# Adding at the destination: one of three folds in a feature-crossing kernel becomes a DMA

## What is computed

```python
x0 = xk = e                                   # (1024, 39, 16)
for W in (f0, f1, f2):                        # (39*39, 128), (128*39, 128), (128*39, 128)
    z = einsum('bfd,bgd->bfgd', x0, xk).reshape(b, f * g, d)
    xk = einsum('bpd,pm->bmd', z, W)          # (1024, 128, 16)
    outs.append(xk)
z = sum(concatenate(outs, axis=1), axis=-1)   # (1024, 384)
h = concatenate([z, dense_ctx], axis=1)       # (1024, 400)
h = maximum(h @ W_top1 + b_top1, 0); h = maximum(h @ W_top2 + b_top2, 0)
y = h @ W_top3
```

## Time and profile before

| | |
|---|---|
| median of 3 runs | 1478.6 us (1476.04 to 1482.9) |
| span of the profiled execution | 1472.1 us (its own time beyond the span is not given) |
| busy: VectorE, ScalarE, GpSimd | 1171.3, 954.1, 1150.0 us |
| chain that ended last, by engine | PE 44%, issue 16%, DVE 15%, POOL 14%, DMA 5% |
| mean granted TensorE clock | 0.966 of full speed (2.4 GHz) |

### The profile page before, as it was taken

One profiled execution on the slowest core, in us unless ns is written; L12 is line 12 of the kernel. 1 busy time (PEld: TensorE's weight loads), 2 busy tenths in 40 slices (PEclk: granted clock), 3 DMA queues, 4 the chain that ended last, 5 costly groups with the idle time before them and its releaser, 6 DMA issues.

```text
span 1472.1 us, 25210 instructions
## 1 busy us (share of the span) xinstructions
PE 1312.5 (89%) x5987; PEld 1044.1 (71%) x5987; DVE 1171.3 (80%) x3210; ACT 954.1 (65%) x3077; POOL 1150.0 (78%) x834
## 2 busy tenths in 40 slices
PE   0259998998989998999989999899989999899998
PEld 0127776786767876788777877688767887788777
DVE  2028998967988698978988699887988789896993
ACT  1117786756766586766867577666867578675783
POOL 7655889977889788978899788997899787674772
PEclk9959999999999999999999999999999999999999
DMA  8132213402233023232133222330233320330200
GB/s 213 19 59 56 48 22 74 79 8 51 51 69 61 3 51 64 59 57 48 19 66 65 37 51 57 64 60 3 52 61 60 57 51 19 74 76 5 49 1 1
DMA packets 62703, 74.33 MB, mean 50 GB/s; under 512 B 25835, under 2 KB 32988, under 8 KB 62538
## 3 DMA queue, kind: packets, MB, share of 16 engines
q1 hardware_dynamic: 52554, 69.88, 22.9%
q0 software_dynamic: 9984, 2.58, 2.0%
HBM read 59.74 MB, written 4.96 MB: 44 GB/s over the span
## 4 chain that ended last, share of the span: by engine, by line
PE 44%; issue 16%; DVE 15%; POOL 14%; DMA 5%; ACT 4%; SPq 1%; another core or an unknown queue 1%; DVEq 1%; ACTq 0%; POOLq 0%
PE pieces L699 10%; PE pieces L701 9%; PE pieces L700 9%; DVE parts L540 9%; POOL emb L311 4%; POOL parts L320 4%; DMA partners<-x_wide 4%; PE xbank L719 3%; ACT parts L406 3%; PE gbank L710 3%; POOL parts L322 2%; DVE pairs L550 2%; PE cur_bank L681 2%; DVE pairs_lo L566 2%; PE cur_bank L682 2%
## 5 line engine op out<-in xcount | busy, mean ns | idle before, releaser
L406 ACT ACTIVATE parts<-pieces,x_cols 128x128 f32<-128x128 f32 x2560 | 721.0, 377 | 193.2 <-PE pieces L701 167.7
L540 DVE SCALAR_TENSOR_TENSOR parts<-pieces,x_cols,parts 128x128 f32<-128x128 f32 x2432 | 679.0, 340 | 141.4 <-PE pieces L701 106.3
L699 PE MATMUL pieces<-w_hi,cur_hi 128*128 128x512 f32 (+1 forms) x1280 | 550.2, 430 | 64.8 <-DVE parts L540 53.1
L701 PE MATMUL pieces<-w_hi,cur_lo 128*128 128x512 f32 (+1 forms) x1280 | 500.5, 391 | 0.0
L700 PE MATMUL pieces<-w_lo,cur_hi 128*128 128x512 f32 (+1 forms) x1280 | 499.7, 390 | 0.0
L320 POOL TENSOR_TENSOR parts<-parts 128x1024 f32<-128x1024 f32 x127 | 325.0, 2559 | 129.8 <-DVE parts L540 127.8
L311 POOL DMA_INDIRECT emb<-in_tbl,next_ids x312 | 325.5, 1043 | 92.4 <-issue 79.8
L699 PEld LDWEIGHTS pieces<-w_hi,cur_hi 128*128 128x128 f32 x1280 | 244.9, 191 | 133.9 <-DVE parts L540 69.3
L420 ACT ACTIVATE pairs_hi<-pairs 117x512 fp32r<-117x512 f32 (+1 forms) x224 | 142.0, 634 | 231.7 <-DVE pairs L550 194.7
L701 PEld LDWEIGHTS pieces<-w_hi,cur_lo 128*128 128x128 f32 x1280 | 243.5, 190 | 50.6
L700 PEld LDWEIGHTS pieces<-w_lo,cur_hi 128*128 128x128 f32 x1280 | 245.2, 192 | 47.1 <-issue 0.4
(11 more groups left out here) (67 smaller groups left out, 712.3 us busy)
## 6 DMA issues: line engine op xcount, KB each, us to landing
partners<-x_wide SPq DMA_DIRECT2D x62, 546.0 KB
partners<-x_wide SPq DMA_DIRECT2D x31, 468.0 KB
x_cols<-emb_rows SPq DMA_DIRECT2D x128, 59.0 KB
emb<-in_tbl,next_ids POOLq DMA_INDIRECT x312
x_wide<-x_rep SPq DMA_DIRECT2D x31, 156.0 KB
wt<-in_wt SPq DMA_DIRECT2D x1, 768.0 KB
wt<-in_wt SPq DMA_DIRECT2D x1, 512.0 KB
partners<-in_w SPq DMA_DIRECT2D x1, 351.0 KB
```

Source lines behind the costliest of these rows:

```text
L406: last = nc.scalar.activation(parts[n % 2][:, 4 * i + r, :], src[:, r * H:(r + 1) * H], ACT.Copy, scale=x_cols[n // 4][:, n % 4, f:f + 1])
L540: nc.vector.scalar_tensor_tensor(acc, src[:, r * H:(r + 1) * H], x_cols[n // 4][:, n % 4, f:f + 1], acc, ALU.mult, ALU.add).then_inc(acc_d ...
L699: nc.tensor.matmul(dst[:, 0:width], hi[:, cols], w1_hi[:, ws], start=True, stop=False)
L701: nc.tensor.matmul(dst[:, 0:width], lo[:, cols], w1_hi[:, ws], start=False, stop=True).then_inc(l2d_ready if q in D_PIECES else l2a_ready, 1)
```

## The change

The addition of 8 onto 8 leaves GpSimd's compute list. In its place GpSimd issues a DMA with an addition at the destination, from `parts[8:16]` to `parts[0:8]`: 128 rows of 4096 bytes. An addition of one number in a scratch buffer stands between the wait for the parts and the issue. The list of a block is now: wait for the parts, issue the fold, gathers, `make_x_diag`, wait for the fold's landing, the two other additions, once a quad the move. `tree_done` counts two additions a block. The last block keeps its addition on VectorE, with a semaphore of its own.

```diff
-TREE = 3
+TREE = 2
...
+        scratch = sb("scratch", [P, 2])
...
-            def add_parts(u, n):
-
-                g, v, out4 = u * BLOCKS + n, parts[n % 2], tails[n % 2]
+            def fold_parts(u, n):
+
+                g, v = u * BLOCKS + n, parts[n % 2]
                 pool.wait_ge(prod_done, (g + 1) * len(A_PIECES))
                 pool.wait_ge(acc_done, (g + 1) * D_OPS)
-                pool.tensor_tensor(v[:, 0:8], v[:, 0:8], v[:, 8:16], ALU.add).then_inc(tree_done, 1)
-                pool.wait_ge(tree_done, g * TREE + 1)
+                pool.tensor_tensor(scratch[:, 0:1], scratch[:, 0:1], scratch[:, 1:2], ALU.add)
+                pool.dma_start(v[:, 0:8], v[:, 8:16], accum_op=ALU.add).then_inc(parts_folded, 16)
+
+            def add_parts(u, n):
+
+                g, v, out4 = u * BLOCKS + n, parts[n % 2], tails[n % 2]
+                pool.wait_ge(parts_folded, (g + 1) * 16)
                 pool.tensor_tensor(v[:, 0:4], v[:, 0:4], v[:, 4:8], ALU.add).then_inc(tree_done, 1)
                 wait(pool, cur2_ready, g - 1)
-                pool.wait_ge(tree_done, g * TREE + 2)
+                pool.wait_ge(tree_done, g * TREE + 1)
                 pool.tensor_tensor(out4[:], v[:, 0:4], v[:, 16:20], ALU.add).then_inc(tree_done, 1)
...
+            pool.memset(scratch[:], 0.0)
...
+                    fold_parts(u, n)
                     for f in shares:
                         gather(u + 1, f)
+                    make_x_diag(u, n)
                     add_parts(u, n)
                     if k == 0 and not last:
                         pool.wait_ge(gathered, (u + 1) * F * 16)
                         pool.wait_ge(rows_copied, u + 1)
                         move_ids(u + 1)
-                    make_x_diag(u, n)
...
             for n in range(BLOCKS - EARLY, BLOCKS - 1):
+                fold_parts(QUADS - 1, n)
+                make_x_diag(QUADS - 1, n)
                 add_parts(QUADS - 1, n)
-                make_x_diag(QUADS - 1, n)
...
-                nc.vector.tensor_tensor(v[:, 0:8], v[:, 0:8], v[:, 8:16], ALU.add).then_inc(tree_done, 1)
-                dve.wait_ge(tree_done, g * TREE + 1)
+                nc.vector.tensor_tensor(v[:, 0:8], v[:, 0:8], v[:, 8:16], ALU.add).then_inc(last_folded, 1)
+                dve.wait_ge(last_folded, 1)
```

More of the change, by code:

```diff
@@ L192, in cin_kernel @@
         prod_done = sem("prod_done")
+        parts_folded = sem("parts_folded")
+        last_folded = sem("last_folded")
         tree_done = sem("tree_done")
@@ L313, in gather @@
                     bass.IndirectOffsetOnAxis(ap=next_ids[:, f:f + 1], axis=0)).then_inc(gathered, 16)
+            def fold_parts(u, n):
+                g, v = u * BLOCKS + n, parts[n % 2]
+                pool.wait_ge(prod_done, (g + 1) * len(A_PIECES))
+                pool.wait_ge(acc_done, (g + 1) * D_OPS)
+                pool.tensor_tensor(scratch[:, 0:1], scratch[:, 0:1], scratch[:, 1:2], ALU.add)
+                pool.dma_start(v[:, 0:8], v[:, 8:16], accum_op=ALU.add).then_inc(parts_folded, 16)
             def add_parts(u, n):
                 g, v, out4 = u * BLOCKS + n, parts[n % 2], tails[n % 2]
-                pool.wait_ge(prod_done, (g + 1) * len(A_PIECES))
-                pool.wait_ge(acc_done, (g + 1) * D_OPS)
-                pool.tensor_tensor(v[:, 0:8], v[:, 0:8], v[:, 8:16], ALU.add).then_inc(tree_done, 1)
-                pool.wait_ge(tree_done, g * TREE + 1)
+                pool.wait_ge(parts_folded, (g + 1) * 16)
                 pool.tensor_tensor(v[:, 0:4], v[:, 0:4], v[:, 4:8], ALU.add).then_inc(tree_done, 1)
                 wait(pool, cur2_ready, g - 1)
-                pool.wait_ge(tree_done, g * TREE + 2)
+                pool.wait_ge(tree_done, g * TREE + 1)
                 pool.tensor_tensor(out4[:], v[:, 0:4], v[:, 16:20], ALU.add).then_inc(tree_done, 1)
@@ L583, in add_last_parts @@
                 dve.wait_ge(acc_done, (g + 1) * D_OPS)
-                nc.vector.tensor_tensor(v[:, 0:8], v[:, 0:8], v[:, 8:16], ALU.add).then_inc(tree_done, 1)
-                dve.wait_ge(tree_done, g * TREE + 1)
+                nc.vector.tensor_tensor(v[:, 0:8], v[:, 0:8], v[:, 8:16], ALU.add).then_inc(last_folded, 1)
+                dve.wait_ge(last_folded, 1)
                 nc.vector.tensor_tensor(v[:, 0:4], v[:, 0:4], v[:, 4:8], ALU.add).then_inc(tree_done, 1)
                 dve.wait_ge(cur2_ready, g - 1)
-                dve.wait_ge(tree_done, g * TREE + 2)
+                dve.wait_ge(tree_done, g * TREE + 1)
                 nc.vector.tensor_tensor(out4[:], v[:, 0:4], v[:, 16:20], ALU.add).then_inc(tree_done, 1)
```

## The result

The changed kernel takes **1633.8 us** (median of 4 runs, 1632.3 to 1634.9) against 1478.9 (median of 4): a ratio of 1.1046, interval 1.1024 to 1.1067. It is 155 us slower, where +26 was forecast, and lies beyond the range given (1460 to 1565). Its profiled execution has a span of 1633.0 us.

The account below looks back on a forecast made before the run. TensorE was taken as busiest but not full (942 of 1000 us), most of its gaps coming from VectorE's waits for `partners`. The terms -16 + 3 + 8 + 31 = +26 gave 1505 us, range 1460 to 1565.

Parts of the forecast that it names:

- The relief, -16: VectorE's pairs and `pairs_lo`: without GpSimd's widest fold 66 of 120 us of lock-outs go, shortening the path by 16 us.
- The landing: The fold's transfer, from issue to arrival: 5.2 us taken for every block, bounds 3.9 to 7.4 us.
- The tree and its due time, +3: GpSimd's additions end 8.9 to 9.5 us after the last part, ScalarE needs them at 9.3: +3 us of a possible 25.
- The order, +8: x_diag ahead of the additions waits for a late `G` product once a quad: 2.3 us late in eight quads, +8 us.
- The collision, +31: The fold's transfer delays the `partners` load VectorE awaits once a quad: 4.5 us in seven quads, +31 us (18 to 53).
- GpSimd becomes the bound: Rival: a landing of 7.4 us or more makes GpSimd's cycle 11.7 us a block over 10.64; 1602 us, chance 0.13.

Follow-up runs that it names:

- e1: Changed kernel without the accumulating transfer and its issue, the widest fold left out of the sum; 1468.7 us, ratio 0.995.
- f4: Changed kernel with GpSimd's order of before: gathers ahead of the transfer, both other additions behind it, x_diag last; 1771.9 us, ratio 1.201.
- k2: Changed kernel with the `partners` loads of the second to eighth quad cut to one row in six or seven; 1549.7 us, ratio 1.048.
- k1: Kernel before the change with the `partners` loads of the second to eighth quad cut to one row in six or seven; 1458.9 us, ratio 0.986.
- f3: Changed kernel with the widest fold a GpSimd addition again, in the order fold, gathers, other additions, x_diag; 1553.7 us, ratio 1.053.
- e5: Changed kernel with the transfer cut to one eighth of its bytes, seven eighths of the widest fold missing; 1523.9 us, ratio 1.031.
- e4: Changed kernel with the fold's transfer on 64 of 128 partitions, the other half of the widest fold missing; 1600.6 us, ratio 1.084.

## Why the prediction was wrong

The prediction's sum was -16 + 3 + 8 + 31. Step by step:

*The relief, -16.* The mechanism was right, its size too large: the pairs' share of the excess fell from 120 to 71 us, where 66 of 120 were to go, and in e1, which has no fold at all and loses no time, only to 85. Besides, x_diag now runs directly ahead of two additions and holds up the halving, in a row (VectorE's timeline in the changed kernel, beside GpSimd's 657.54 to 659.54 above):

```profile
657.66 2.17 DVE L605 TENSOR_TENSOR tails<-tails 128x256 f32<-128x256 f32 x1
...
668.72 0.41 DVE L605 TENSOR_TENSOR tails<-tails 128x256 f32<-128x256 f32 x1
```

2.17 us instead of 0.41. Of 126.7 us of excess 110.9 remain; by the fit the relief is 9 us, not 16. This is a matter of size, and not what broke the forecast.

*The landing.* Taken as 5.2 us everywhere (3.9 to 7.4). It is 3.7 to 3.8 us from the issue to the next addition where nothing runs beside it, below the low end, and 8 to 11 us in one block of each tile, where a `partners` load does (4 to 6 in its neighbours), above the high end. One figure for all blocks was wrong on both sides. The two-column addition took 0.41 us, not 0.2; the issue 0.94, within its bounds.

The Trainium skill's fit (DMA: Bandwidth & Descriptors, section Anatomy of one DMA), from which the prediction worked out an estimate of 3.2 us, is near the free landing of 3.8 us of f4; for landings beside a load it has no term, and these cost 64 us or more.

*The tree and its due time, +3: the step that failed first.* The tree was forecast at 8.9 to 9.5 us, and the free one took 9.6. But its due time, 9.3 us, was read from one block, and being late was priced at 0.2 us a block. Every block of a quad has its own due time. Counted from the last part to the start of ScalarE's first piece two blocks on, as means over the second to seventh quad of the kernel before, it is 6.6 us for the eleventh block of a quad, 8.7 to 9.1 for five others and 14.1 for the third. In the same quads k2's trees end behind k1's due times in seven blocks of sixteen above all, by 1.2 to 3.6 us, some 15 us a quad in all; the third block's share, 2.3 us, is what the order's term foresaw. That is without collisions: the tree went from 7.2 to 10.2 us, ScalarE's waits for `tails` from 4 to 102 us, and the time of these six quads rose by 58 us, 9.6 a quad. That it rose by less than 15 may come from a late block moving the due time of the next ones; this is not shown. The prediction's first three terms, -16 + 3 + 8 = -5 for all eight quads, stand against it. e1 has the same order without transfer and issue and loses nothing, so the 58 us belong to the transfer and the steps around it.

*The order, +8.* With the transfer the order is worth 141 us (296 against 155), as cover. Alone, with the addition, it costs 124. The two do not add up: 296 + 124 would be 420, and together they cost 155. The prediction costed the gathers' move at nothing as long as they arrive in time; f3, where no landing needs cover, shows 78 us for it.

*The collision, +31: right in kind, wrong in its victim.* The load of `partners` hardly suffers (+15 us in six waits); the fold does. It should have been asked of both transfers: which one is queued behind the other, and who waits for that one? Once a quad VectorE waits for `partners`, but in every tile GpSimd waits for the fold. In the second to seventh quad the collisions measured 61 us, some 10 a quad where 4.5 were forecast, and in all 64 us or more.

*The rivals.* "GpSimd becomes the bound", 1602 us at a chance of 0.13, is nearest: its signs (GpSimd waiting for the landing, ScalarE for `tails`) are what the profile shows. Its condition, a landing of 6.3 us or more throughout, did not hold, and GpSimd still waited 84 times for the parts, so it is not simply the bound; in f4 it is. That its 1602 us come near the 1633.8 measured is therefore in part luck. The range cut off most of that case.

## What to carry to other kernels

When an operation between two buffers' release is replaced by a transfer, add up the whole time from the last input to the release, free and beside every other load, and compare it with the due time of every block, not of one: here a tree that was in time for most blocks was late for seven of sixteen. Ask of a collision which of the two transfers waits, and cost the engine that waits for that one. An issue and the steps around it cost GpSimd 1.3 us here, half of the addition that was to be saved, so a transfer frees an engine only as far as the engine need not wait for it.

## What the runs showed of the hardware

*A transfer beside another queue's load waits, even a small one.* In e5 only 64 KB move, in rows of 512 bytes, and free of loads the addition behind one starts 1.5 us after the end of the issue (issue at 743.17 for 0.96 us, addition at 745.65). Two of its folds, the first disturbed by a load issued at 619.53, the second by one issued at 656.02 (timeline of GpSimd, e5):

```profile
626.61 0.96 POOL L324 DMA_DIRECT2D parts<-parts  x1
633.91 1.26 POOL L330 TENSOR_TENSOR parts<-parts 128x512 f32<-128x512 f32 x1 [2.92 <-DMA parts<-parts]
...
660.80 0.96 POOL L324 DMA_DIRECT2D parts<-parts  x1
669.37 2.06 POOL L330 TENSOR_TENSOR parts<-parts 128x512 f32<-128x512 f32 x1 [2.19 <-DMA parts<-parts]
```

From the end of the issue to the next addition 6.3 and 7.6 us pass, against 10.9 for eight times the bytes. In the changed kernel's trace such a fold starts about 24 of its 128 packets of 4 KB in the first three microseconds after the issue, next to none in the following one or two, and the rest as the load's packets run out; with the loads cut (k2, from the second quad on) no landing takes over 5.6 us. A packet itself takes as long as in a free fold (336 to 368 ns against 347). The Trainium skill (DMA: Bandwidth & Descriptors, section Issuing engines are not separate DMA queues) says that transfers of all issuers end on the same 16 engines and interleave. The trace agrees that the two hinder each other, but shows no even interleaving: the later, smaller transfer waits for most of the load.

*Adding at the destination took little more time a byte than the copies did.* DMA queues of the changed kernel:

```profile
q0 software_dynamic: 28272, 69.17, 23.5%
q1 hardware_dynamic: 52554, 69.88, 20.8%
```

Less the gathers' 2.58 MB and 2.0% of 1472.1 us, the folds moved 66.6 MB in 16 x (383.8 - 29.4) us, which is 85 engine-us a MB, where the copies of the first queue take 78 here and took 77 before. The two are not alike: the fold has rows of 4 KB within the core's own memory, the copies mostly rows of 2 KB and less. And on 64 partitions (e4) the adding packets took 617 ns in the mean instead of 351, so 151 engine-us a MB instead of 86.

*A small VectorE operation can be held by several GpSimd operations in a row*: the halving of 0.41 us took 2.17, from 657.66 to 659.83, while x_diag and the addition behind it ran from 657.54 to 659.54. The Trainium skill (Trainium Architecture — The Big Picture, section What this means for kernel authors) calls the port pair of the two engines an exclusive lock; the trace agrees.

*TensorE can pay a gap twice.* The granted clock over the thousand microseconds fell from 0.98 to 0.94, and 0.85 in the stretch of the disturbed fold, in which TensorE was busy 5.62 of 12 us. After a gap of 7.47 us that ended at 636.05 the granted clock was 0.50 from 635 to 639 and 1.00 from 641 to 645 (the chain in order of time of the changed kernel, behind a transfer of `partners` that ended at 634.15):

```profile
622.11 12.04 DMA partners<-x_wide
...
638.98 0.43 PE pieces L710
...
642.49 0.23 PE pieces L710
```

0.43 us and 0.23 us for a matmul of the same line, which is the lower and the higher of the two levels, 1.2 and 2.4 GHz.
